# A mixture-of-experts layer on one core: a second pair of down buffers, and another order of work where the shared experts' gate stage ends

## The reference, cut to what matters

```python
# 32 experts, 8 of them per token; I = 512, SI = 1024
top_k_index = top_k(masked, 8)                     # experts of each token
gate = ragged_dot(xs, w_gate, group_sizes)         # (rows of expert) x 1024 x 512
up   = ragged_dot(xs, w_up, group_sizes)
down = ragged_dot(silu(gate) * up, w_down, group_sizes)   # x 512 x 1024
routed = (down[unsort].reshape(T, K, H) * tkw[..., None]).sum(axis=1)
shared = silu(x @ sw_gate) * (x @ sw_up) @ sw_down        # 1024 x 1024 each
return routed + shared
```

## Time and profile before

| what | us |
|---|---|
| median of 3 runs | 13044.12 (13040.3 to 13050.17) |
| the profiled execution | 13069.08 |
| its span, first to last instruction | 13067.2 |
| TensorE's granted clock over it | 0.993 of full |
| pairs, gate stage, from about | 2198 to 3449 |
| expert tiles | 3457 to 12447 |
| pairs, down stage | to 13060 |

### The profile page before, as it was taken

The page is one execution under the profiler, slowest core; times in us unless marked ns, Lnnn a source line. Parts: engine busy times, 40 slices in busy tenths (PEclk is TensorE's granted clock), DMA queues, the critical chain, the costliest instruction groups (busy, mean ns, idle before and its releaser), DMA issues.

```text
span 13067.2 us, 199937 instructions
## 1 busy us (share of the span) xinstructions
PE 12853.3 (98%) x58200; PEld 10686.0 (82%) x58201; DVE 6366.4 (49%) x7627; ACT 3504.4 (27%) x4781; POOL 7205.9 (55%) x7206
## 2 busy tenths in 40 slices
PE   9999998999999999999999999999999999999999
PEld 7888887888788888888888888888778788888888
DVE  6888887777533333343333433333443433333366
ACT  4444443333212212221212211222222211211132
POOL 6688875120256656665656655666656655655500
PEclk9999999999999999999999999999999999999999
DMA  4544444343445545565545654555665644544554
GB/s 150 157 124 120 117 127 106 83 118 84 104 97 116 116 97 116 116 142 106 133 97 116 138 114 97 133 128 140 147 147 116 167 97 97 110 97 97 105 161 156
DMA packets 1080150, 1564.13 MB, mean 120 GB/s; under 512 B 176581, under 2 KB 590017, under 8 KB 1079938
## 3 DMA queue, kind: packets, MB, share of 16 engines
q0 software_dynamic: 318112, 587.24, 25.7%
q1 hardware_dynamic: 370866, 689.25, 17.3%
q10 hardware_dynamic: 390960, 284.86, 8.1%
HBM read 995.67 MB, written 590.68 MB: 121 GB/s over the span
## 4 chain that ended last, share of the span: by engine, by line
PE 78%; issue 1%; DMA 1%; DVE 1%; ACT 1%; ACTq 0%; DVEq 0%; POOL 0%; POOLq 0%; SPq 0%
PE gps L1982 22%; PE ups L1982 22%; PE yps L1982 22%; PE xt L1946 6%; PE gps L1946 4%; PE hp L1946 4%; DMA hsd<-sig 1%; DVE wlo L1627 0%; DMA raw<-in_w_gu_dram 0%; DVEq L1137 0%; DMA xg<-xnd,xidx 0%; DMA hz<-hsd 0%; DVE xl L1627 0%; ACT whi L1492 0%; ACT whi L1497 0%
## 5 line engine op out<-in xcount | busy, mean ns | idle before, releaser
L1337 POOL DMA_INDIRECT x2d<-yrow,yidx x1086 | 1927.0, 1774 | 2554.6 <-DVE yrow L1836 2114.2
L1319 POOL DMA_INDIRECT xg<-xnd,xidx x2172 | 2186.6, 1007 | 989.4 <-issue 532.1
L1847 DVE TENSOR_TENSOR hp<-sig,ups 128x512 f32<-128x512 f32 x543 | 378.0, 696 | 3442.3 <-ACT sig L1543 2130.3
L1982 PE MATMUL gps<-whi,xh 128*128 128x512 f32 x4344 | 1692.7, 390 | 49.8 <-DVE xl L1627 43.1
L1982 PE MATMUL ups<-whi,xh 128*128 128x512 f32 x4344 | 1691.7, 389 | 0.0
L1982 PE MATMUL ups<-wlo,xh 128*128 128x512 f32 x4344 | 1691.5, 389 | 0.0
L1982 PE MATMUL gps<-wlo,xh 128*128 128x512 f32 x4344 | 1691.5, 389 | 0.0
L1982 PE MATMUL gps<-whi,xl 128*128 128x512 f32 x4344 | 1691.5, 389 | 0.0
L1982 PE MATMUL ups<-whi,xl 128*128 128x512 f32 x4344 | 1691.4, 389 | 0.0
L1982 PE MATMUL yps<-whi,xh 128*128 128x512 f32 x4344 | 1345.8, 391 | 46.3 <-DVE xl L1627 46.3
L1982 PE MATMUL yps<-wlo,xh 128*128 128x512 f32 x4344 | 1343.1, 390 | 0.0
(11 more groups left out here) (253 smaller groups left out, 24149.5 us busy)
## 6 DMA issues: line engine op xcount, KB each, us to landing
hsd<-sig ACTq DMA_DIRECT2D x2172, 64.0 KB
hz<-hsd ACTq DMA_DIRECT2D x543, 256.0 KB
raw<-in_w_gu_dram SPq DMA_DIRECT2D x128, 1024.0 KB
xg<-xnd SPq DMA_DIRECT2D x512, 128.0 KB
kT<-in_ctx_dram SPq DMA_DIRECT2D x64, 704.0 KB, 8.6
xg<-xnd,xidx POOLq DMA_INDIRECT x2172
xnd<-xn SPq DMA_DIRECT2D x65, 512.0 KB, 4.2
xin<-in_x_dram SPq DMA_DIRECT2D x64, 512.0 KB
```

Of the source, the lines that this page charges most:

```text
L1319: pool.indirect_dma_start(out=xg[:, i, q, :], out_offset=None, in_=quarter_rows, in_offset=bass.IndirectOffsetOnAxis(ap=xidx[i][:, q:q + 1 ...
L1337: pool.indirect_dma_start(out=half_rows, in_=yrow[:, i, a * 512:(a + 1) * 512], in_offset=None, out_offset=bass.IndirectOffsetOnAxis(ap=yi ...
L1847: dve.tensor_tensor(hp, hb, ups, ALU.mult).then_inc(h_done, 1)
L1982: ins = pe.matmul(ps, rows, w[:, i, :], start=first and n == 0, stop=last_one and n == 2)
```

## The change: what it does

1. The weights' buffers get other places. The high and low parts have six slots each (they had seven); T3's high part and T4's low part of the pairs lie in a region `back`, B22's raw unit and `xT` in a region `front`. Behind the pairs the same bytes are `down_raw`, four units: two pairs of down buffers, chosen by the expert's parity. ACT and DVE read the pair's index from a constant table (`down_units`).
2. SP issues the down units of expert e when those of e-1 have landed and those of e-2 have been split; before, when those of e-1 had been split. The four gate units of e still stand ahead of them in the queue. Expert 1's down units are issued ahead of its gate units.
3. In the last pair step one gate unit more is split (three instead of two), each one place earlier; `x_turn` and the split of the first tile's rows stand ahead of `give_1`; `give_2` is cut into `multiply_2` and `turn_2`, and `multiply_2` stands ahead of the split of gate unit 3.
4. In the last tile the split of the shared down weights' first unit stands behind Silu, and that of the first rows behind `spread_h`.

```diff
-        whi = sb("whi", [P, OPS, STRIPS, STRIP], F32R)
-        wlo = sb("wlo", [P, OPS, STRIPS, STRIP], F32R)
-        raw = sb("raw", [P, 5, STRIPS, STRIP])
-        xT = sb("xT", [P, 2, KX, P])
+        whi = sb("whi", [P, UNITS, STRIPS, STRIP], F32R)
+        wlo = sb("wlo", [P, UNITS, STRIPS, STRIP], F32R)
+        raw = sb("raw", [P, GU, STRIPS, STRIP])
+        with ExitStack() as pairs_only:
+            front = pairs_only.enter_context(nc.sbuf_tensor("front", [P, DN, STRIPS, STRIP], F32))
+            back = pairs_only.enter_context(nc.sbuf_tensor("back", [P, DN, STRIPS, STRIP], F32R))
+        down_raw = sb("down_raw", [P, 2 * DN, STRIPS, STRIP])
...
+        op_hi = {o: whi[:, i, :, :] for i, o in enumerate((B21, B11, T1, T2, B22, T4))}
+        op_hi[T3] = back[:, 0, :, :]
+        op_lo = {o: wlo[:, o, :, :] for o in range(UNITS)}
+        op_lo[T4] = back[:, 1, :, :]
+        op_raw = [front[:, 0, :, :] if i == GU else raw[:, i, :, :] for i in RAW_OF]
+        xT_flat = front[:, 1, :, :].rearrange("p k x -> p (k x)")
+        xT = xT_flat.rearrange("p (i k t) -> p i k t", i=2, t=P)
...
+        def down_units(eng, e):
+
+            first = eng.value_load(con[0:1, bass.ds(C_TURN + e, 1)].bitcast(I32), min_val=0, max_val=DN)
+            return [down_raw[:, bass.ds(first + q, 1), :, :].rearrange("p o k x -> p (o k) x") for q in range(DN)]
...
-            def load_expert_unit(e, q):
-                unit = A["w_gu"][bass.ds(e * GU + q, 1)] if q < GU else A["w_dn"][bass.ds(e * DN + q - GU, 1)]
-                sp.dma_start(units[q], unit.rearrange("o j p x -> p (o j) x")).then_inc(w_ld[q], 16)
+            def load_gate_unit(e, q):
+                unit = A["w_gu"][bass.ds(e * GU + q, 1)]
+                sp.dma_start(raw[:, q, :, :], unit.rearrange("o j p x -> p (o j) x")).then_inc(w_ld[q], 16)
+
+            def load_down_unit(e, slot, q):
+                unit = A["w_dn"][bass.ds(e * DN + q, 1)]
+                sp.dma_start(down_raw[:, DN * slot + q, :, :], unit.rearrange("o j p x -> p (o j) x"))\
+                    .then_inc(w_ld[GU + q], 16)
...
-                    for q in range(UNITS - 1):
-                        load_expert_unit(0, q)
+                    for q in range(GU):
+                        load_gate_unit(0, q)
+                    load_down_unit(0, 0, 0)
                 if p.at(GATES - 1):
                     sp.wait_ge(x_lo, split_at(T4, GATES))
-                    load_expert_unit(0, UNITS - 1)
+                    load_down_unit(0, 0, 1)
...
-            with sp.Fori(1, E) as e:
-                for q in range(UNITS):
-                    if q < GU:
+            sp.wait_ge(done, done_at(T4, GATES))
+            for q in range(DN):
+                sp.wait_ge(w_ld[GU + q], 16)
+                load_down_unit(1, 1, q)
+            for q in range(GU):
+                sp.wait_ge(lo_gu, q + 1)
+                load_gate_unit(1, q)
+            with sp.Fori(0, (E - 2) // 2) as turn:
+                for slot in range(2):
+                    e = 2 * turn + 2 + slot
+                    for q in range(GU):
                         sp.wait_ge(lo_gu, GU * (e - 1) + q + 1)
-                    else:
-                        sp.wait_ge(lo_dn, DN * (e - 1) + q - GU + 1)
-                    load_expert_unit(e, q)
+                        load_gate_unit(e, q)
+                    for q in range(DN):
+                        sp.wait_ge(w_ld[GU + q], 16 * e)
+                    for q in range(DN):
+                        sp.wait_ge(lo_dn, DN * (e - 2) + q + 1)
+                        load_down_unit(e, slot, q)
...
-            sp.wait_ge(lo_dn, DN * (E - 1) + 1)
+            sp.wait_ge(lo_dn, DN * (E - 2) + 1)
             load_unit(B22, 2)
-            sp.wait_ge(lo_dn, DN * E)
+            sp.wait_ge(lo_dn, DN * (E - 1))
...
+                if over:
+                    split_gu(0, range(1))
                 keep_1(p)
                 if t is not None:
                     w_high(B11, t)
                 if over:
-                    split_gu(0, range(1))
+                    split_gu(0, range(1, 2))
                 high(T3, p)
                 keep_5(p)
                 if t is not None:
                     w_high(T1, t)
                 if over:
-                    split_gu(0, range(1, 2))
+                    split_gu(0, range(2, 3))
...
-                    split_gu(0, range(2, GU))
+                    split_gu(0, range(3, GU))
+                    x_high(0)
...
             def split_dn(e):
+                down_unit = down_units(act, e)
                 for q in range(DN):
                     act.wait_ge(w_ld[GU + q], 16 * (e + 1))
-                    act.activation(whi[:, GU + q + 1, :, :], units[GU + q], ACT.Copy).then_inc(hi_dn, 1)
+                    act.activation(whi[:, GU + q, :, :], down_unit[q], ACT.Copy).then_inc(hi_dn, 1)
...
-            def give_2(n):
+            def multiply_2(n):
                 dve.wait_ge(a_read, n + 1)
                 dve.wait_ge(u3_read, n + 1)
                 dve.tensor_tensor(kept_5[False], silu_2, kept_5[False], ALU.mult).then_inc(product_2, 1)
+
+            def turn_2(n):
...
                 sum_12(p)
+                if over:
+                    x_turn(0, 0, 0)
+                    sum_22(p)
+                    xt_low(0)
                 give_1(n)
                 if t is not None:
                     w_low(B22, t)
-                sum_22(p)
+                if not over:
+                    sum_22(p)
...
             walk_gates(dve, gate_step)
-            x_turn(0, 0, 0)
-            xt_low(0)
-            split_gu(0, range(2, GU))
+            multiply_2(GATES - 1)
+            split_gu(0, range(3, GU))
             x_turn(1, 1, 0)
-            give_2(GATES - 1)
+            turn_2(GATES - 1)
```

More of the change, by code:

```diff
@@ L94, in constants @@
     c[:, C_QUAD] = p // SQ
+    c.view(np.int32)[:, C_TURN:C_TURN + E] = DN * (np.arange(E) % 2)
     blank = np.zeros((1, P, 2), np.int32)
@@ L1374, in w_high @@
                 act.wait_ge(u_ld[RAW_OF[o]], load_at(o, t + 1))
-                if t == 2 and o:
-                    if o < T3:
+                if t == 2:
+                    if o < B22:
                         act.wait_ge(gu_mm, EXPERT_TILES)
+                    elif o == T3:
+                        act.wait_ge(lo_dn, DN * (E - 1) + 1)
                     else:
@@ L1381, in w_high @@
                     wait(act, done, done_at(o, t * DUOS))
-                act.activation(whi[:, o, :, :], raw[:, RAW_OF[o], :, :], ACT.Copy).then_inc(w_hi, 1)
+                act.activation(op_hi[o], op_raw[o], ACT.Copy).then_inc(w_hi, 1)
             def high(o, p, k=0):
@@ L1490, in split_gu @@
                     if isinstance(e, int):
-                        act.wait_ge(done, done_at(q + 1, GATES))
-                    act.activation(whi[:, q + 1, :, :], units[q], ACT.Copy).then_inc(hi_gu, 1)
+                        act.wait_ge(done, done_at(q, GATES))
+                    act.activation(whi[:, q, :, :], raw[:, q, :, :], ACT.Copy).then_inc(hi_gu, 1)
             def split_dn(e):
+                down_unit = down_units(act, e)
                 for q in range(DN):
                     act.wait_ge(w_ld[GU + q], 16 * (e + 1))
-                    act.activation(whi[:, GU + q + 1, :, :], units[GU + q], ACT.Copy).then_inc(hi_dn, 1)
+                    act.activation(whi[:, GU + q, :, :], down_unit[q], ACT.Copy).then_inc(hi_dn, 1)
             def x_high(t):
@@ L1543, in tile @@
                 act.activation(hb, gps, ACT.Silu).then_inc(silu_done, 1)
+                if last:
+                    w_high(B21, 2)
                 if c.on(1):
@@ L1546, in tile @@
                     new_weights(act, c, 1, lambda e: split_gu(e, range(1, GU)))
+                spread_h(t, c.slot())
                 if last:
                     high(B21, dense, 1)
-                spread_h(t, c.slot())
-                if last:
                     w_high(B11, 2)
@@ L1636, in w_low @@
                         dve.wait_ge(down_mm, EXPERT_TILES)
+                    else:
+                        dve.wait_ge(lo_dn, DN * E)
                 else:
                     wait(dve, done, done_at(o, t * DUOS))
-                low(wlo[:, o, :, :], raw[:, RAW_OF[o], :, :], whi[:, o, :, :]).then_inc(w_lo, 1)
+                low(op_lo[o], op_raw[o], op_hi[o]).then_inc(w_lo, 1)
             def x_low(o, p, k=0):
@@ L1713, in gate_step @@
                 if p.on(-1):
-                    give_2(n - 1)
+                    multiply_2(n - 1)
+                    turn_2(n - 1)
                 if p.turn() is not None:
@@ L1804, in split_gu @@
                         dve.wait_ge(done, done_at(q, GATES))
-                    low(wlo[:, q, :, :], units[q], whi[:, q + 1, :, :]).then_inc(lo_gu, 1)
+                    low(wlo[:, q, :, :], raw[:, q, :, :], whi[:, q, :, :]).then_inc(lo_gu, 1)
             def split_dn(e):
+                down_unit = down_units(dve, e)
```

(6 more changed lines are left out.)

18 lines of the change are left out of this document (7 added, 11 removed).

## The result

| | before | after |
|---|---|---|
| median | 13046.07 us (4 runs, 13040.30 to 13050.17) | 13136.95 us (4 runs, 13131.61 to 13137.75) |
| profiled execution, its span | 13069.08, 13067.2 | 13137.75, 13135.8 |
| feed-forward part (first pair product to the end) | 10869.5 | 10965.2 |

The changed kernel is slower: ratio 1.0069, 95% interval 1.0052 to 1.0087, 91 us by the medians (before has one run more here than in the table of the start). The forecast was 13104 us, with 13145 as the upper end of its range. The two profiled executions differ by only 69 us, because the one of before entered the pairs at 2197.7 us and the one of after at 2170.6, in a part that the change doesn't touch. Behind that point after is 95.7 us longer.

A forecast was written before the change was run, and what follows sets the result against it. PE was taken to bound the kernel, busy for 98% of the span, so only its pauses could change. Terms -37 + 89 + 8 + 0 = +60 us on 13044 gave 13104 us, range 12990 to 13145.

The forecast's parts named there:

- Plain first tiles: First tiles of 13 large experts: early down loads run over the `hsd` to `hz` trip, 6.85 us per expert, +89 us.
- -37 for the pairs: Three pairs of one-tile experts: stops at `gate_up` and slow clock behind them go, less +10.5 us for trips, net -37 us.
- +8 for the lone ones: Four single one-tile experts: loaded own trips, +2.5 us each, less about 2 us at a short expert, +8 us.
- its load is over by then, -4.5: Expert behind a one-tile expert: its trip, loaded before, was taken to be free after the change, -4.5 us.
- The three stops: PE's waits ahead of `gate_up` at the three pairs of one-tile experts, 39.7 us in all, expected to go.
- The one-tile expert's own trip: Hidden rows' trip in a one-tile expert's tile: unloaded before, loaded after, 4.7 us more and a slow clock, +7 us.
- The gate stage's end: Last pair step: earlier `multiply_2` wins 5.2 us, first tile's loaded trip costs about 5; sum 0, ends -8 and +4.
- The first window: Sign: stretch 3484 to 5780 on PE, free of pauses before, some 28 us longer with four first tiles.
- `gps`: Sign: PE's waits "gps until xl", ahead of `gate_up`, a few us instead of 43.1.
- `yps`: Sign: PE's waits "yps until xl", ahead of `down`, about 25 waits and 90 us instead of 46.
- Early loads are free: Rival, 20%: down units load in other queues' gaps and hold up no trip; -60 us, 12984 us.
- Half the delay: Rival, 12%: large experts' first-tile trips take 6.83 us, +39 us against -40, 13043 us.
- The stops stay too: Rival, 15%: each stop at pairs of one-tile experts keeps 8 or 9 us, about +27 us on top, 13131 us.

The follow-up runs named there:

- e1: Changed kernel, but down units again wait for the split of expert e-1's down units, expert 1's behind its gate units: 13080.49 us, ratio to before 1.002.
- e7: Changed kernel, but in SP's queue an expert's down units stand ahead of its gate units: 13079.58 us, ratio to before 1.0019.
- e5: Changed kernel, but ACT splits the down units ahead of issuing `hz` instead of behind it: 13046.38 us, ratio to before 0.9994.
- e3: Changed kernel, but SP waits for expert e-1's down splits where e-1 has two tiles or more: 13045.90 us, ratio to before 0.9993.
- e6: Kernel before, plus one register load, its value unused, on ACT and on DVE ahead of the down splits: 13067.19 us, ratio to before 1.001.
- e4: e1 with the order of the gate stage's end undone as well: 13078.22 us, ratio to before 1.0017.
- e10: Kernel before with only ACT's down split moved ahead of issuing `hz`: 13030.56 us, ratio to before 0.9984.
- e11: Kernel before with ACT's down split ahead of issuing `hz` and DVE's `right_rows` and down split ahead of `x_turn`: 13061.05 us, ratio to before 0.9986.
- e12: e8 run once more, beside e11 on the same chip: 13054.36 us, ratio to before 0.9981.
- e8: Changed kernel with ACT's down split ahead of issuing `hz` and DVE's `right_rows` and down split ahead of `x_turn`: 13022.70 us, ratio to before 0.9976.
- e2: Changed kernel, but from expert 2 on half of each down unit isn't loaded, so results differ: 13091.31 us, ratio to before 1.0029.

## Why the prediction was right, and where its terms were off

The direction, the main mechanism and the range held, the range by 8 us only: 13136.95 under 13145. What filled its upper part wasn't the plain tiles, for which it was kept, but mostly the tiles behind one-tile experts. By its steps:

- **Plain first tiles, forecast +89 us, measured +96.9.** Right in kind: stretch 3484 to 5780 is 29 us too long (forecast 28), trips 8.6 to 10.2 us with a mean of 9.5 (forecast 8.9), the 13 pauses sum to 70.0 us or 5.4 each, 5.2 by the profile (forecast 4.55), and the clock behind them costs 2.1 each (forecast 2.3). I chose 8.9 below the loaded row of 9.62; the row itself was nearer. In the row shown, the load's 2.17 MB fell into 4034 to 4044, wholly on the trip. e1 and e7 show that the place of the load is the cause; e5 shows that most of it is paid because the splits stand behind `hz` on ACT: with them ahead of it, the cost is 29.9 us instead of 96.9.
- **One-tile experts, forecast -37 for the pairs and +8 for the lone ones, measured +0.9 in all.** This is the step that failed. The three stops did go (39.7 us), as e3 confirms too. The one-tile expert's own trip was right in size: I gave it 4.7 us, and the pauses grew by 4.6 us at the four lone ones and 4.8 at the first of each pair. What was wrong stands in the prediction as "its load is over by then, -4.5" for the expert behind, and as 1 us for the second one of a pair. After the change such a trip carries the load of the next expert's down units, like that of every plain first tile. This is the first tile behind the one-tile expert at 6258 of before, in after, then SP's queue within that trip, 6276.45 to 6285.68:

```profile
6272.44 2.57 SPq L1212 DMA_DIRECT2D down_raw<-in_w_dn_dram  x2
...
6276.45 1.77 ACTq L1547 DMA_DIRECT2D hsd<-sig  x4
...
6285.68 0.35 ACTq L1555 DMA_DIRECT2D hz<-hsd  x1
```

```profile
q1 hardware_dynamic: 1312, 2.60, 76.2%
```

  The seven trips behind one-tile experts take 8.8 to 9.3 us (9.1 to 9.8 before), not 4.2. Those tiles, with the second tile of one of the experts, lose 26.4 us instead of 39.7: a gain of 13 where 7 x 4.5 = 31.5 was forecast. The three second ones of the pairs have trips of 8.5 to 8.8 us (3.2 before) and lose 19.4 us instead of 1.0: 18 where 3 was forecast. So the pairs gain 20 us and not 37, and the lone ones cost 21 and not 10. e3 confirms the cause: it holds the next down units back from the tiles behind, and their loss is 0. The other leg of the trip wasn't in my sum either: at the ten one-tile experts `hz` lands 6.3 to 7.3 us behind its issue, against 2.6 to 3.4 in the plain first tiles, and ACT waits for it 0.04 to 1.1 us behind the splits. Nor was the register load at these experts, where the forecast charged it only to the large ones; e6 prices it at 13 us in the old kernel, most of it here. The own trips' 4.6 to 4.8 us contain both, so that this term came out so near is in part luck.
- **The gate stage's end, forecast 0 (ends -8 and +4): right.** The wait for the product fell from 6.75 to 1.6, and the first tile's pause with its clock rose from 0.8 to 8.2 us, +3 us in sum with the pairs' last step below; e4 agrees within 2 us.
- **The sum, +60 against +91 by the medians.** The terms measured are +96.9 and +0.9, the first tile's +7.4, the pairs' last step -4.4, and -4.9 at two short experts (tiles that waited 2.3 and 2.6 us before and don't now): +95.9, which is the 95.7 of the feed-forward part. What the forecast lacks of it is 25 at the one-tile and short experts (-4.0 against -29), 8 in the plain tiles and 3 at the gate stage's end. That the profile of before was 25 us above its median was told in the forecast; its mix stage, 2197.7 us, was 17 us or more longer than that of after and of e1 to e10 (2170.6 to 2180.5; the lot of e11 and e12 has longer ones again), so the difference of the two profiled executions alone, 69 us, would have understated the change.
- **Its signs, and small slips.** The first window (29 us for 28), `gps` (3.4) and the 8 to 10 us from `hsd` to `hz` came as told. "About 25 waits and 90 us" for `yps` came out at 32 and 148.4; the forecast's own terms, 46.3 and 13 x 4.55, already made 105. Six units in 22 us are 3.7 us a unit and not 3.5, and the free case, 12984 us, lies below the range's lower end of 12990 that was to reach to it. Neither moves the sum.
- **The rivals.** *Early loads are free* is ruled out by the 9.5 us trips, and by e1, which lies 26 us above before where after lies 91. *Half the delay* is ruled out by the same trips, none of the 13 under 8.5 us. *The stops stay too* gave nearly the right time, 13131 us, for the wrong reason: PE's `gps` wait is 3.4 us, so they went. A like amount, 28 us over the forecast of these tiles, was paid in `down` instead, where loaded trips of 8.2 to 9.3 us stand. No run shows that the two are equal for more than chance. The rule of the Trainium skill ("DMA: Bandwidth & Descriptors", Rules for kernel authors) to issue a DMA early and to wait for it late didn't make the change free: it cost 91 us. e8 shows an order of work in which the same early loads come out 31 us below before.

## What to carry to other kernels

A load that is issued earlier also lands somewhere else: look at what small, dependent transfers run in the place it moves to, and count both legs of a trip. Where a load moves away, ask which load comes into its place: the forecast's largest miss was a trip that it took to be free. Before adding a buffer, look at what stands between the arrival and the use on each engine's queue: here one call moved on ACT gave the kernel before 23 us with no memory at all, while the second pair of buffers, with the order unchanged, cost most of 91. In these kernels it paid to put the work that needs nothing from a trip between its issue and the wait for it.

## What was not expected of the hardware

- How much a load on the other queue holds up a small round trip: with 0.07 MB from SP's queue beside it 4.2 us (and 1.06 MB from POOL's), with half of the down units (e2) 7.3 to 8.0, with 2.2 MB 9.5. In the loaded trip SP's queue held 59.7% of the engines' time and POOL's 37.6%.
- A register load of 0.28 us on ACT and 0.30 on DVE costs the whole kernel 13.4 us by the medians (e6; interval of the ratio 1.0000 to 1.0019, so from nothing to 25 us) at 32 experts, although ACT is idle for 73% of the span and DVE for 51%: it stands on the way from `hz` to `down`. Nearly all of it shows at one-tile and short experts, and 0.7 us in the 13 plain tiles.
- A pause of 5.9 us is followed by 16 matmuls in 5.28 us, PEclk 0.68, where 3.63 would do. This is the window on PE of after:

```profile
4053.82:4059.10 5.28, 5.28 (x16) 0.68 0.41 100
```

  Of the 13 plain tiles' cost, 27 of 96.9 us is this clock and not the pause.
